# Gram matrices of two samples per matmul, another order of the pieces, and gathers without the wait for gram matrices

## The chip, the cores and the metric

The kernel runs on one core of a Trainium2 chip. A core has TensorE (PE in the rows; matmuls), VectorE (DVE), ScalarE (ACT), GpSimd (POOL) and SyncE (SP), each with its own instruction queue, worked off in order, and 16 DMA engines. Engines wait for each other through semaphores only. The metric is the device time of one execution in microseconds. Here it is 626.21 us (median of 3 runs, 625.28 to 627.51).

## What is computed

For each of 2048 rows, 26 table rows of 64 floats are gathered, projected to 128 and layer-normed, mixed from 26 to 32 features and layer-normed again. With the projected dense row they are 33 vectors of 128. All their pairwise products go through a linear layer with layer norm, and three dense layers follow. All is fp32. Cut to what matters:

```
e = stack([tbl_f[ids[:, f]] for f in range(26)], axis=1)          # (2048, 26, 64)
x = layer_norm(dense @ Wd.T, gd, bd)                              # (2048, 128)
y = layer_norm(einsum('bnd,ed->bne', e, Ws), gs, bs)
y = layer_norm(einsum('bne,pn->bep', y, Wsi), gsi, bsi)           # (2048, 128, 32)
T = concatenate([x[:, None, :], swapaxes(y, 1, 2)], axis=1)       # (2048, 33, 128)
Z = einsum('bnd,bmd->bnm', T, T)
out = layer_norm(Z[:, TRIL_I, TRIL_J] @ Wl.T, gl, bl)             # first 384 of 512 kept
h = relu(concatenate([out, dense], axis=1) @ W_top1 + b_top1)
h = relu(h @ W_top2 + b_top2)
return h @ W_top3
```

## The kernel before

The 2048 rows are 16 tiles of 128. Each tile passes a pipeline of stages, and the program is one loop over "quarters" `h`. A stage that runs once per tile has a number `at`: it runs for tile t in quarter `h = 4t + at` (`tile(h, at)`). A stage that runs in four parts (four batches of features, or four pieces of 32 rows each) runs part k in quarter `4t + at + k` (`part(h, at)`). So four quarters are one tile, and in each quarter every engine does its share for several tiles at once. The order of the calls in the loop body of an engine is the order of that engine's queue. Written out for one tile:

- GpSimd gathers the 26 features by one indirect DMA each (L255), in batches of 8, 6, 6, 6, into one of two buffers `emb`. Before a batch of tile t it waits that the tile two before has been normalized (`nrm_ready`), and that a gram piece has been done (`gram_done`).
- Measuring (part at 1): TensorE transposes a batch (L312), ScalarE copies it (`embt`), TensorE multiplies with a weight gram matrix (L321), VectorE multiplies with `emb` and sums (L757, L761): variances. ScalarE takes the root.
- VectorE normalizes a half of the features (L778, 7 or 6 instructions of two features, written into `nrm` with feature as the fastest index) and shuffles them by 32x32 transposes into `byn` (L788, two instructions), in quarter 5.
- Pieces (part at 6): TensorE mixes (L330), ScalarE copies (`mixed`, L505), TensorE projects (L342), VectorE adds the bias (L793), ScalarE squares (L510), VectorE sums (L800), ScalarE takes the root (L515); in the next quarter VectorE takes the reciprocal (L805) and scales into `V` (L811).
- Gram matrices (part at 7): for each of 32 samples of a piece, one matmul of 32 stationary and 34 moving columns (L354), four samples side by side in four column groups of the array. ScalarE copies the result to `zs` (L521).
- By sample (at 12): VectorE transposes `zs` to `zb` (L822 to L825), TensorE transposes on (L384 to L388), ScalarE copies `zt`. Interact (at 13, L396): the big layer, 5 matmuls of 512 columns. ScalarE squares and scales (`z`), TensorE transposes back (at 15, L404).
- Layer 1 in two halves (at 18 and 19, L418), layer 2 (at 20, L425), layer 3 (at 21, L434), store (at 22). There are 4 * 15 + 23 = 83 quarters.

Each matmul of the source is two instructions of the trace, a transpose is one. The weights are prepared during quarters 0 to 10 (`prepare_...`, `fold`).

## Time and profile before

| | us |
|---|---|
| median of 3 runs | 626.21 |
| the profiled execution | 628.74 |
| its span, first to last instruction | 626.9 |
| TensorE busy in the span | 520.4 |
| VectorE busy | 519.8 |
| ScalarE busy | 295.3 |
| GpSimd busy (making gathers) | 402.9 |

The profiled execution is 2.5 us above the median, and its span 1.8 us below its own time. Two engines are each busy for 83% of the span. The chain of work that ended last is 37% TensorE, 24% VectorE, 16% time without a wait that the profile shows, 8% ScalarE and 8% GpSimd. GpSimd's busy time leaves out a pause of 0.30 us that follows each gather.

### The profile page before, as it was taken

What the parts mean: (1) busy time and instruction counts of PE and PEld (TensorE: products, weight loads), DVE (VectorE), ACT (ScalarE), POOL (GpSimd) and SP (SyncE); (2) the same over time, 40 slices, a digit from 0 to 9 for tenths busy, and PEclk for the clock granted to TensorE, in tenths of its full rate; (3) what the DMA queues carried; (4) which work ended last, traced back from release to release, by engine and by line L of the source; (5) the groups of instructions that cost most, each with busy time, mean ns of one, the idle gap of its engine ahead of it and who ended that gap; (6) DMA issues with size and microseconds to landing.
All of it is one profiled execution on the core that took longest, in us unless ns stands there. A gap on an engine that the chain in (4) does not pass through costs nothing.

```text
span 626.9 us, 17592 instructions
## 1 busy us (share of the span) xinstructions
PE 520.4 (83%) x6955; PEld 394.3 (63%) x6955; DVE 519.8 (83%) x1073; ACT 295.3 (47%) x730; POOL 402.9 (64%) x422
## 2 busy tenths in 40 slices
PE   1462777777899999999998899899998989979886
PEld 1352556545576767676767677676776676747665
DVE  3499689899999999999998979999999898986500
ACT  0410343445465556464636445555555464635422
POOL 6777775767777777777777777777777777200000
PEclk9955887798999999999999899999999999999999
DMA  7311111111111111111111111111111111000000
GB/s 176 109 24 33 27 28 30 28 34 27 35 28 36 28 37 27 37 28 31 34 28 36 29 36 27 37 27 37 28 36 28 29 27 28 14 1 2 2 1 1
DMA packets 22610, 20.22 MB, mean 32 GB/s; under 512 B 12017, under 2 KB 14721, under 8 KB 22529
## 3 DMA queue, kind: packets, MB, share of 16 engines
q0 software_dynamic: 13312, 13.66, 12.1%
q1 hardware_dynamic: 8400, 4.33, 2.7%
q8 instruction: 55, 0.90, 0.6%
q10 hardware_dynamic: 816, 1.11, 0.6%
q14 instruction: 27, 0.21, 0.1%
HBM read 19.07 MB, written 0.01 MB: 30 GB/s over the span
## 4 chain that ended last, share of the span: by engine, by line
PE 37%; DVE 24%; issue 16%; ACT 8%; POOL 8%; DMA 3%; SPq 2%; ACTq 0%; DVEq 0%; POOLq 0%
PE b_l L418 10%; POOL emb L255 8%; PE b_y L342 7%; PE b_l L396 5%; DVE nrm L778 3%; DVE byn L788 3%; DVE V L811 3%; DVE yb L793 3%; DVE var_y L800 3%; PE b_a L321 3%; PE b_z L354 3%; DVE prod L757 2%; DMA emb<-in_tbl,idx 2%; ACT mixed L505 2%; PE b_a L312 2%
## 5 line engine op out<-in xcount | busy, mean ns | idle before, releaser
L255 POOL DMA_INDIRECT emb<-in_tbl,idx x416 | 402.2, 967 | 134.7 <-issue 118.5
L510 ACT ACTIVATE sq<-yb 128x1024 f32<-128x1024 f32 x64 | 67.7, 1059 | 191.1 <-DVE yb L793 187.2
L342 PE MATMUL b_y<-mixed,projw 64*128 64x512 f32 x256 | 74.9, 663 | 23.8 <-ACT mixed L505 23.8
L793 DVE TENSOR_TENSOR yb<-b_y,bias_y 128x1024 f32<-128x1024 f32 x64 | 78.1, 1220 | 19.9 <-PE b_y L342 19.5
L811 DVE TENSOR_TENSOR V<-yb,rstd_y 128x256 f32<-128x256 f32 x256 | 91.9, 422 | 2.2
L800 DVE TENSOR_REDUCE var_y<-sq 128x32 f32<-128x1024 f32 x64 | 77.8, 1215 | 6.9 <-ACT sq L510 5.6
L396 PE MATMUL b_l<-wlt,zt 128*128 128x512 f32 x160 | 72.9, 603 | 0.5 <-ACT zt L561 0.5
L330 PE MATMUL b_mix<-mix,byn 128*128 128x128 f32 x512 | 72.4, 287 | 0.0
L321 PE MATMUL b_a<-gram_w,embt 128*128 128x128 f32 x416 | 66.3, 303 | 6.3 <-ACT embt L494 5.6
L354 PE MATMUL b_z<-V 128*32 128x34 f32 x4096 | 58.2, 200 | 12.5 <-DVE V L811 9.7
L330 PEld LDWEIGHTS b_mix<-mix,byn 128*128 128x128 f32 x512 | 66.4, 203 | 0.2
L354 PEld LDWEIGHTS b_z<-V 128*32 128x32 f32 x4096 | 49.1, 110 | 24.9 <-DVE V L811 9.3
L321 PEld LDWEIGHTS b_a<-gram_w,embt 128*128 128x128 f32 x416 | 57.5, 211 | 11.5 <-ACT embt L494 10.2
L788 DVE STREAM_TRANSPOSE byn<-nrm 128x1024 f32<-128x1024 f32 x32 | 59.3, 1927 | 0.5
L312 PE MATMUL b_a<-ident,emb 128*128 128x128 f32 x208 | 38.5, 303 | 22.4 <-DVE prod L757 16.1
L494 ACT ACTIVATE embt<-b_a 128x512 f32<-128x512 f32 (+1 forms) x64 | 33.0, 516 | 49.6 <-PE b_a L312 49.3
L396 PEld LDWEIGHTS b_l<-wlt,zt 128*128 128x128 f32 x160 | 29.1, 190 | 42.9 <-issue 42.1
L418 PE MATMUL b_l<-z_t,w 128*128 128x128 f32 x384 | 54.1, 278 | 0.0
L778 DVE TENSOR_TENSOR nrm<-emb,rstd_n 128x128 f32<-128x128 f32 x208 | 51.9, 384 | 1.1
L418 PEld LDWEIGHTS b_l<-z_t,w 128*128 128x128 f32 x384 | 48.9, 195 | 0.0
L418 PE MATMUL b_l<-dt,w 128*128 128x128 f32 x256 | 41.6, 286 | 0.9 <-ACT y_sb L596 0.9
L312 PEld LDWEIGHTS b_a<-ident,emb 128*128 128x128 f32 x208 | 25.6, 153 | 26.0 <-issue 18.1
(131 smaller groups left out, 681.7 us busy)
## 6 DMA issues: line engine op xcount, KB each, us to landing
emb<-in_tbl,idx POOLq DMA_INDIRECT x416
dense<-in_r_dense_t SPq DMA_DIRECT2D x16, 128.0 KB, 2.3
...
out_y<-y_sb SPq DMA_DIRECT2D x16, 0.5 KB
...
```

What stands on the lines that cost most here:

```text
L255: pool.indirect_dma_start(out=emb[t % 2][:, f, :], out_offset=None, in_=tables[f], in_offset=bass.IndirectOffsetOnAxis(ap=idx[:, t, f:f + ...
L312: last = nc.tensor.transpose(b_a[:, n * P:(n + 1) * P], emb[t % 2][:, 2 * c:2 * c + 2, :].rearrange("p n d -> p (n d)"), ident[:, :])
L321: last = nc.tensor.matmul(b_a[:, n * P:(n + 1) * P], embt[:, n, :], gram_w[:, :], start=True, stop=True)
L330: last = nc.tensor.matmul(b_mix[:, m * P:(m + 1) * P], byn[t % 2][:, j:j + 2, :].rearrange("p j d -> p (j d)"), mix[:, :], start=True, sto ...
L342: last = nc.tensor.matmul(b_y[:, j2, :], projw[r, :], mixed[c % 2][r, :], start=True, stop=True, tile_position=(64 * j2, 0))
L354: last = nc.tensor.matmul(b_z[32 * q:32 * q + 32, GRAM * j:GRAM * (j + 1)], v[:, 0:NP], v, start=True, stop=True)
L396: last = nc.tensor.matmul(b_l1[:, :], zt[:, c, :], wlt[:, c, :], start=(c == 0), stop=(c == RC - 1))
L418: last = nc.tensor.matmul(dst, w1[:, c, m * P:(m + 1) * P], rhs, start=(n == 0), stop=(n == 4))
L788: nc.vector.transpose(byn[t % 2][:, :, d].rearrange("p j d -> p d j"), nrm[:, d, :]).then_inc(byn_ready, 1)
L793: nc.vector.tensor_tensor(yb[c % 2][:, :, :, :].rearrange("e h s p -> e (h s) p"), b_y[:, :, :].rearrange("e h (s p) -> e (h s) p", p=NP), ...
L800: nc.vector.tensor_reduce(var_y[c % 2][:, :], sq[:, :, :, :].rearrange("e h s p -> e (h s) p"), AXX, ALU.add).then_inc(vary_done, 1)
L811: last = nc.vector.tensor_tensor(V[t % 2][:, j2, c, m:m + 2, :, 0:NP].rearrange("e m q p -> e (m q) p"), yb[c % 2][:, j2, 4 * m:4 * m + 8, :],
```

## The change

- **Gathers** (GpSimd): no wait for `gram_done` any more; a wait for `nrm_ready` remains at the first feature of each half.
- **Gram matrices**: `V` holds two samples side by side (68 columns). One matmul has 64 stationary and 68 moving columns; of the 2x2 blocks the two diagonal ones are used. 16 matmuls per piece in two column groups, where 32 in four were. Their result is in two PSUM banks. ScalarE copies it by 4 instructions on 32 partitions each, where one on 128 was, and writes the dense row's share into `V` by 4 instructions where one was. To make room, the bank `b_l0` is now the bank `b_x`.
- **Layouts**: `nrm` and `zs` have the transposed order of their free dimensions. So L778 writes contiguous runs, and the 32x32 transposes read with a stride. The third transpose of `by_sample` has 128 columns, where 64 were, and TensorE adds its two halves by an accumulating matmul (`pair_x`).
- **Order**: shuffle at 4 (was 5), mix at 5 (was 6), scale in the quarter of its piece, by_sample and pairs at 11 (was 12), interact at 12 (13), back at 14 (15), both halves of layer 1 and layer 2 at 15 (18, 19 and 20), layer 3 at 16 (21), store at 18 (22). 79 quarters. The order within a quarter is new on TensorE, ScalarE and VectorE.

```diff
-        nrm = sb("nrm", [P, D, NP])
+        nrm = sb("nrm", [P, NP, D])
...
-        V = [sb(f"V{h}", [P, 2, 4, 4, NQ, GRAM]) for h in range(2)]
-        zs = [sb(f"zs{h}", [P, GRAM, NJ]) for h in range(2)]
-        zb = sb("zb", [P, ZB_X + 2 * NP])
+        V = [sb(f"V{h}", [P, 4, 2, 4, 2, PAIRED]) for h in range(2)]
+        zs = [sb(f"zs{h}", [P, NJ, SLOTS]) for h in range(2)]
+        zb = sb("zb", [P, ZB_X + 4 * NP])
...
+        b_l0 = b_x
...
-                for b in range(4):
-                    after(pool, nrm_ready, 2 * (t - 2) + b // 2 + 1)
-
-                    after(pool, gram_done, 4 * t + b - PROJECT - 2)
-                    for f in features(b):
-                        pool.indirect_dma_start(out=emb[t % 2][:, f, :], out_offset=None, in_=tables[f],
-                                                in_offset=bass.IndirectOffsetOnAxis(ap=idx[:, t, f:f + 1], axis=0)
-                                                ).then_inc(gathered[t % 2][b], 16)
+                for f in range(NF):
+                    if f in (HALVES[0][0], HALVES[1][0]):
+                        after(pool, nrm_ready, 2 * (t - 2) + (f > 0) + 1)
+                    b = next(b for b in range(4) if f in features(b))
+                    pool.indirect_dma_start(out=emb[t % 2][:, f, :], out_offset=None, in_=tables[f],
+                                            in_offset=bass.IndirectOffsetOnAxis(ap=idx[:, t, f:f + 1], axis=0)
+                                            ).then_inc(gathered[t % 2][b], 16)
...
-                    for q in range(NQ):
-                        v = V[t % 2][:, j % 2, c, j // 2, q, :]
-                        last = nc.tensor.matmul(b_z[32 * q:32 * q + 32, GRAM * j:GRAM * (j + 1)], v[:, 0:NP], v, start=True, stop=True)
+                    for q in range(2):
+                        v = V[t % 2][:, c, j % 2, j // 2, q, :]
+                        last = nc.tensor.matmul(b_z[64 * q:64 * q + 64, j // 4, PAIRED * (j % 4):PAIRED * (j % 4 + 1)], v[:, 2:2 + 2 * NP], v,
+                                                start=True, stop=True, tile_position=(0, 64 * q))
...
+            def pair_x(t):
+                pe.wait_ge(zt_copied, 2 * t + 1)
+                pe.wait_ge(x_copied, 2 * (t + 1))
+                for k in range(2):
+                    nc.tensor.matmul(b_x[0:64, 0:P], zb[:, ZB_X + 64 * k:ZB_X + 64 * (k + 1)], ident[:, :], start=(k == 0), stop=(k == 1),
+                                     tile_position=(0, 0))
...
-                after(pe, h1_relued, 4 * (t - 1) + 2)
-                after(pe, y_copied, t - 1)
+                pe.wait_ge(xn_done, min(t + 4, T))
+                after(pe, y_copied, t)
...
-                    pe.wait_ge(zt_copied, 2 * min(t + 2, T))
-                    after(pe, y_copied, t)
-                else:
-                    pe.wait_ge(z_ready, min(t + 2, T))
+                    pe.wait_ge(x_copied, 2 * min(t + 4, T))
...
-                if (t := tile(h, DENSE_BACK)) is not None:
+                if (x := part(h, 1)):
+                    transposes(*x)
+                if (x := part(h, 6)):
+                    project(*x)
...
+                if (t := tile(h, 14)) is not None:
+                    interact_back(t)
...
+                if (x := part(h, 5)):
+                    mix_features(*x)
+                if (t := tile(h, 15)) is not None:
+                    layer1(t, 0)
...
+                if (t := tile(h, 15)) is not None:
+                    layer1(t, 1)
+                if (x := part(h, 7)):
+                    gram(*x)
...
+                if (t := tile(h, 12)) is not None:
+                    interact(t)
...
-                if (t := tile(h, PAIRS)) is not None:
-                    pair_rows(t)
-                if (t := tile(h, INTERACT)) is not None:
-                    interact(t)
-                if (t := tile(h, LAYER3)) is not None:
-                    layer3(t)
-                if (t := tile(h, LAYER1)) is not None:
-                    layer1(t, 0)
-                if (t := tile(h, INTERACT_BACK)) is not None:
-                    interact_back(t)
-                if (t := tile(h, LAYER1 + 1)) is not None:
-                    layer1(t, 1)
...
-                nc.scalar.activation(zs[t % 2][:, :, 8 * c:8 * c + 8].rearrange("p c j -> p j c"),
-                                     b_z[:, 0:8 * GRAM].rearrange("p (j c) -> p j c", c=GRAM), ACT.Copy).then_inc(zs_copied, 1)
+                for q in range(NQ):
+                    r, slot, first = slice(32 * q, 32 * q + 32), 2 * (q % 2), GRAM * (q % 2)
+                    last = nc.scalar.activation(
+                        zs[t % 2][r, 8 * c:8 * c + 8, slot:slot + GRAM].rearrange("p (a j) c -> p a j c", a=2),
+                        b_z[r, :, 0:4 * PAIRED].rearrange("p a (j c) -> p a j c", c=PAIRED)[:, :, :, first:first + GRAM], ACT.Copy)
+                last.then_inc(zs_copied, 1)
...
-                nc.scalar.activation(V[t % 2][:, :, :, :, :, NP].rearrange("e h c m q -> e q (c m) h"),
-                                     src.rearrange("e (q a h) -> e q a h", q=NQ, h=2), ACT.Identity, scale=gd[:, 0:1], bias=bd[:, 0:1]
-                                     ).then_inc(x_copied, 1)
+                for q in range(NQ):
+                    last = nc.scalar.activation(V[t % 2][:, :, :, :, q // 2, 2 * (NP + 1) * (q % 2)].rearrange("e c h m -> e c m h"),
+                                                src[:, 32 * q:32 * q + 32].rearrange("e (c m h) -> e c m h", m=4, h=2),
+                                                ACT.Identity, scale=gd[:, 0:1], bias=bd[:, 0:1])
+                last.then_inc(x_copied, 1)
...
-                    last = nc.vector.tensor_tensor(nrm[:, :, f:f + 2].rearrange("p d n -> p n d"), emb[t % 2][:, f:f + 2, :],
+                    last = nc.vector.tensor_tensor(nrm[:, f:f + 2, :], emb[t % 2][:, f:f + 2, :],
...
-                for k in range(2):
-                    d = slice(k * D // 2, (k + 1) * D // 2)
-                    nc.vector.transpose(byn[t % 2][:, :, d].rearrange("p j d -> p d j"), nrm[:, d, :]).then_inc(byn_ready, 1)
+                d = slice(k * D // 2, (k + 1) * D // 2)
+                nc.vector.transpose(byn[t % 2][:, :, d].rearrange("p j d -> p d j"), nrm[:, :, d].rearrange("p n d -> p d n")).then_inc(byn_ready, 1)
...
+                if (x := half(h, 2)):
+                    bound_n(*x)
...
+                if (x := part(h, 6)):
+                    scale(*x)
...
+                if (t := tile(h, 4)) is not None:
+                    shuffle(t, 0)
+                    shuffle(t, 1)
```

Three places in the order of the queues. First TensorE at the end of the program, the last two tiles' layers. L396 is interact, L434 layer 3, L418 layer 1, L404 the transposes back, L425 layer 2. Before:

```order
L396 MATMUL b_l<-wlt,zt 128x512 x5
L434 MATMUL b_l<-h,w3p 128x128 x2
L418 MATMUL b_l<-dt,w 128x128 x2
L418 MATMUL b_l<-z_t,w 128x128 x3
L418 MATMUL b_l<-dt,w 128x128 x2
L418 MATMUL b_l<-z_t,w 128x128 x3
L404 MATMUL b_l<-ident,z 128x128 x3
L418 MATMUL b_l<-dt,w 128x128 x2
L418 MATMUL b_l<-z_t,w 128x128 x3
```

and now, where L383, L390 and L392 are the pair transposes, L400 interact, L408 back, L419 layer 1, L426 layer 2, L434 layer 3:

```order
L383 MATMUL b_x<-ident,zb 128x128 x4
L426 MATMUL b_l<-h,w 128x128 x8
L390 MATMUL b_x<-ident,zb 64x128 x2
L392 MATMUL b_x<-xt,ones 32x128
L434 MATMUL b_x<-h,w3p 128x128 x2
L400 MATMUL b_l<-wlt,zt 128x512 x5
L408 MATMUL b_x<-ident,z 128x128 x3
L419 MATMUL b_x<-dt,w 128x128 x2
L419 MATMUL b_x<-z_t,w 128x128 x3
```

Before, all of layer 1 of tile 14 (the four L418 rows behind L434, and the four behind L404) stands behind the last tile's interact. Now even its layer 2 and layer 3 (the rows L426 and L434) stand ahead of it, and behind it follow only the last tile's own layers.

Second VectorE in the middle of the program, in the quarter in which a tile is shuffled. Before:

```order
L800 TENSOR_REDUCE var_y<-sq 128x32
L774 RECIPROCAL rstd_n<-std_n 128x12
L778 TENSOR_TENSOR nrm<-emb,rstd_n 128x2x64 x6
L788 STREAM_TRANSPOSE byn<-nrm 128x32x32 x2
L805 RECIPROCAL rstd_y<-std_y 128x32
L811 TENSOR_TENSOR V<-yb,rstd_y 128x8x32 x4
L793 TENSOR_TENSOR yb<-b_y,bias_y 128x1024
L757 TENSOR_TENSOR prod<-b_a,emb 128x512
```

and now, with L832, L803, L811, L837, L843 and L820 for L800, L774, L778, L805, L811 and L788:

```order
L832 TENSOR_REDUCE var_y<-sq 128x32
L803 RECIPROCAL rstd_n<-std_n 128x12
L811 TENSOR_TENSOR nrm<-emb,rstd_n 128x128 x6
L837 RECIPROCAL rstd_y<-std_y 128x32
L843 TENSOR_TENSOR V<-yb,rstd_y 128x4x64 x4
L820 STREAM_TRANSPOSE byn<-nrm 128x32x32 x2
L825 TENSOR_TENSOR yb<-b_y,bias_y 128x1024
L787 TENSOR_TENSOR prod<-b_a,emb 128x512
```

The scaling of the piece (`V`) moved from behind the two shuffle transposes to ahead of them, and `yb` of the next quarter now stands right behind them.

Third ScalarE in the quarter in which the dense row is written to `V`. Before:

```order
L551 ACTIVATE V<-b_x,bd,gd 128x4x16x2
L554 ACTIVATE xt<-b_x,bd,gd 128x128
L494 ACTIVATE embt<-b_a 128x384
L515 ACTIVATE std_y<-var_y,eps 128x32
L505 ACTIVATE mixed<-b_mix 128x512
L521 ACTIVATE zs<-b_z 128x8x34
L510 ACTIVATE sq<-yb 128x1024
L500 ACTIVATE std_n<-var_m,eps 128x12
L592 ACTIVATE h<-b_l,b 128x128 x2
```

and now:

```order
L503 ACTIVATE embt<-b_a 128x384
L567 ACTIVATE V<-b_x,bd,gd 128x4x4x2 x4
L571 ACTIVATE xt<-b_x,bd,gd 128x128
L532 ACTIVATE zs<-b_z 32x8x34 x4
L607 ACTIVATE h<-b_x,b1p 128x128 x2
L519 ACTIVATE sq<-yb 128x1024
L607 ACTIVATE h<-b_l,b1p 128x128 x2
L576 ACTIVATE zt<-b_x 128x512
L514 ACTIVATE mixed<-b_mix 128x512
L524 ACTIVATE std_y<-var_y,eps 128x32
```

Ahead of the square of the piece (`sq`, L510, now L519) stood six instructions, `mixed` among them. Now ten copies and the first half of layer 1 (`h`, L607) stand ahead of it, and `mixed` has moved behind it, behind the second half of layer 1 and `zt`.

## Rows read from the trace of the kernel before

**Rows 1.** The page's part 2, GpSimd: busy tenths in 40 slices of the span.

```profile
POOL 6777775767777777777777777777777777200000
```

**Rows 2.** Waits of GpSimd over the span: us in total, times, longest us.

```profile
POOL emb L255 <- issue: 118.5, 388, 0.6
POOL emb L255 <- PE b_z L354: 14.3, 26, 3.6
```

**Rows 3.** Timeline of GpSimd: start us, us, engine, line, what [idle before <-releaser].

```profile
3.08 1.10 POOL L255 DMA_INDIRECT emb<-in_tbl,idx  x1 [1.61 <-DMA idx<-in_ids]
...
99.53 0.94 POOL L255 DMA_INDIRECT emb<-in_tbl,idx  x1 [3.63 <-PE b_z L354]
...
175.74 1.03 POOL L255 DMA_INDIRECT emb<-in_tbl,idx  x1 [1.50 <-PE b_z L354]
...
537.31 1.11 POOL L255 DMA_INDIRECT emb<-in_tbl,idx  x1 [0.30 <-issue]
```

**Rows 4.** Windows, one tile and the end: us, busy of PE, PEld, DVE, ACT, POOL, PEclk.

```profile
427.80:460.40 32.60, 30.43 (x435) 23.03 (x431) 30.58 (x62) 18.38 (x45) 24.68 (x27) 1.00 0.16 32
541.80:625.40 83.60, 70.05 (x850) 53.57 (x849) 38.42 (x71) 33.28 (x83) 0.00 (x0) 0.98 0.01 1
```

**Rows 5.** Timeline of TensorE, steady state, then the last batch and the end.

```profile
435.05 0.77 PE L354 MATMUL b_z<-V 128*32 128x34 f32 x64
...
439.74 0.61 PE L418 MATMUL b_l<-dt,w 128*128 128x128 f32 x4
...
442.07 0.98 PE L354 MATMUL b_z<-V 128*32 128x34 f32 x64
...
447.09 2.05 PE L425 MATMUL b_l<-h,w 128*128 128x128 f32 x16
...
454.51 4.56 PE L396 MATMUL b_l<-wlt,zt 128*128 128x512 f32 x10
...
541.81 0.49 PE L312 MATMUL b_a<-ident,emb 128*128 128x128 f32 x3
...
624.37 0.71 PE L434 MATMUL b_l<-h,w3p 128*128 128x128 f32 x4 [0.72 <-ACT h L592]
```

**Rows 6.** Timeline of VectorE, one quarter with a shuffle.

```profile
447.20 1.23 DVE L793 TENSOR_TENSOR yb<-b_y,bias_y 128x1024 f32<-128x1024 f32 x1
448.35 0.55 DVE L757 TENSOR_TENSOR prod<-b_a,emb 128x384 f32<-128x384 f32 x1
...
449.60 1.22 DVE L800 TENSOR_REDUCE var_y<-sq 128x32 f32<-128x1024 f32 x1
450.73 0.22 DVE L774 RECIPROCAL rstd_n<-std_n 128x12 f32<-128x12 f32 x1
450.99 1.58 DVE L778 TENSOR_TENSOR nrm<-emb,rstd_n 128x128 f32<-128x128 f32 x6
452.60 3.80 DVE L788 STREAM_TRANSPOSE byn<-nrm 128x1024 f32<-128x1024 f32 x2
456.27 0.28 DVE L805 RECIPROCAL rstd_y<-std_y 128x32 f32<-128x32 f32 x1
...
457.93 1.22 DVE L793 TENSOR_TENSOR yb<-b_y,bias_y 128x1024 f32<-128x1024 f32 x1
```

**Rows 7.** Groups by line, VectorE with small and with strided operands: busy us, mean ns.

```profile
L714 DVE TENSOR_REDUCE u<-V 128x64 f32<-128x1024 f32 x2 | 3.8, 1896 | 0.1
L825 DVE STREAM_TRANSPOSE zb<-zs 128x64 f32<-128x64 f32 x16 | 3.2, 202 | 0.0
```

**Rows 8.** Groups by line, ScalarE's copies: busy us, mean ns.

```profile
L521 ACT ACTIVATE zs<-b_z 128x272 f32<-128x272 f32 x64 | 41.0, 641 | 0.0
L505 ACT ACTIVATE mixed<-b_mix 128x512 f32<-128x512 f32 x64 | 37.6, 588 | 7.3 <-PE b_mix L330 6.4
L551 ACT ACTIVATE V<-b_x,bd,gd 128x128 f32<-128x128 f32 x16 | 9.4, 588 | 7.3 <-PE b_x L377 7.3
L580 ACT ACTIVATE z_t<-b_l 128x384 f32<-128x384 f32 x16 | 7.8, 490 | 10.7 <-PE b_l L418 10.7
```

300 lines of the change are left out of this document (159 added, 141 removed).

## The prediction, made before the result was known

> **What bounds the kernel now.** I read four views, in this order. The slices of GpSimd [rows 1] are level at 7 tenths up to slice 34 and empty after it. So there are two parts: one in which gathers are made, up to some 540 us, and an end without any. GpSimd's waits [rows 2] say how full the first part is. A gather takes 0.94 us or a little more and is followed by a pause of 0.30 us, which the waits call "issue". The waits for a gram matrix (PE b_z) hold that same pause: 14.3 - 26 x 0.30 = 6.5 us is real waiting. The timeline has the largest, 3.63 us at 99.53, and the last that is more than the pause, 1.50 us at 175.74 [rows 3]. From the first gather (3.08) to the start of the last (537.31) it is 534.2 us for 415 steps, 1.287 us each; without the 6.5 us it is 1.272, or 33.1 us per tile of 26. The third view, one tile in the steady state [rows 4], shows that the other engines just keep up: 32.6 us, TensorE busy for 30.4 of it, VectorE for 30.6. So in the first part three engines are bound at once, and the gathers come first. The last batch's transposes start at 541.81 us [rows 5], 4.5 us after the start of the last gather: the engines are at GpSimd's heels. The fourth view is the end [rows 4]: 83.6 us from there to the end of TensorE's work, TensorE busy for 70.05 of it. It is the part that a new order can shorten.
>
> **The wait of the gathers.** Removed: at most 6.5 us, all of it before 180 us. What waits remain, on `nrm_ready`, don't bind: two buffers are some 33 us of lead, and a half is normalized two or three quarters, about 20 us, behind its gathers. The last gather then starts at 537.3 - 6.5 = 530.8, and its transposes at 535.3 if the engines follow as closely. That is a floor of this kernel: no order of the others gets below it.
>
> **Gram matrices.** In layer 1 twenty instructions of 128 moving columns take 442.07 - 439.74 = 2.33 us [rows 5], 0.91 ns a column. A gram piece is 64 instructions of 34 columns in 0.7 to 0.98 us [rows 5], 11 to 15 ns each, where one alone would stream for 31: between two and three of the four column groups run at once. Now it is 32 instructions of 68 columns, 62 ns each, in two groups: 32 x 62 / 2 = 0.99 us if both groups are full. Bounds: 0.4 us, if it is the number of instructions that counts, and 1.98 us, if the groups don't overlap. I take 1.0, since the row is a matter of columns in two or three groups: +0.2 us a piece.
>
> The Trainium skill (TensorEngine Tiling (Array Packing), Instruction Overhead) says that a matmul has an overhead of some 60 cycles, so that one column costs as much as 60. By it half the instructions would halve a piece, 0.4 us, and the forecast would be about 2 us lower. The rows of this trace, at 11 to 15 ns an instruction, don't show such a floor in four groups.
>
> **ScalarE.** A copy of 272 elements takes 641 ns now, with a strided write [rows 8]. From 384 elements in 490 and 512 in 588 ns [rows 8], 0.77 ns an element, 272 contiguous ones take 0.40 us, and four overlapped some 1.25 us: +0.6 a piece. Bounds 1.2 and 4 x 0.64 = 2.6. The copy to `V`, 588 ns now, becomes four of 32 elements: some 1.1 us, bounds 0.6 and 2.4. ScalarE goes from 18.4 busy us per tile [rows 4] to 21.3, far from the bound, but its queue couples the others.
>
> **VectorE.** L778 writes contiguous runs: 1.61 us for six [rows 6], of which I take off 0.2; 0.4 us a tile. The shuffle's read gets a stride of 256 bytes. A transpose of 64 elements, contiguous on both sides, takes 202 ns, and two of 1024 take 3.67 us [rows 6, 7], 1.8 ns an element in both cases, although the latter write with a stride. So transposes run at some 1.8 ns whatever the layout, and I take 0 for the strided read. The other bound is a reduction: over strided data 1896 ns [rows 7], over contiguous 1.22 us [rows 6], both 1024 elements, +0.68 us. That would be 1.4 us for the shuffle and 0.7 for `by_sample`.
>
> The Trainium skill (SBUF — State Buffer, the note on cachelines under Door 1) speaks against this part: an access that leaves its 16-byte line pays. It is the rule behind the fourth case below, 2.1 us a tile. The strided reduction agrees with it, the transposes with a strided write don't.
>
> **A lap of the steady state.** The sums aren't enough, since order decides. I follow one tile, from the start of the quarter with layer 1 (0), by the starts of the rows [rows 5, 6] and the new order. TensorE: project waits for `mixed` at 1.3, ends 2.4; norms 3.2, mix 4.1, layer 1 8.7, gram 9.7, pair rows 10.1, layer 2 12.0, pair_x 12.8 (with 0.3 for its second matmul). Next quarter: transposes and project, 14.2. VectorE: bias 1.15, norms and bound 1.25, variance 1.15, normalize 1.55, scale 1.7, shuffle 3.7: 24.7 (24.6 with the gain of L778). Meanwhile TensorE has done interact (4.4 us) by 22.1. Next quarter on VectorE: bias, norms and variance 3.6, 0.3 of waiting, scale 1.7: 30.3. Then bias to 31.45, ScalarE squares by 32.7, `mixed` by 33.55, and the next lap's project starts where 1.3 was. **32.2 us a lap**, to which I add 0.3 for small gaps: 32.5. GpSimd needs 33.1. So the engines follow still, with 0.6 us a tile to catch up; and the quarter with layer 1, where the square stands behind it, costs nothing yet, since the chain runs over TensorE there.
>
> The weights' preparation fills VectorE until some 128 us, as before; tile 3's first transposes, which without waits could run at 114, start at about 127. From there 12 laps and 22.9 us to the last batch: 127 + 12 x 32.5 + 22.9 = 540. The floor of the gathers was 535. I take **540**, 1.8 us earlier than now.
>
> **The end.** Same hand work from the last batch's transposes (0). VectorE has shuffled tile 15 by 12.0. Pieces then cost VectorE 5.4 us each (bias 1.15, square 1.1, variance 1.15, root 0.35, scale 1.7): 17.4, 22.8. The third has layer 1 of tile 13 in its quarter, 31.4; the fourth is at 37.3. Interact of tile 14 ends 38.7, and the last piece follows it: project 39.8, scaled 45.1, gram 46.2. Then TensorE alone: layer 1 of tile 14 50.8, pairs and layer 2 53.8, layer 3 and interact 58.8, norm, back and copy 61.5, layer 1 66.1, layer 2 with two copies 69.4, layer 3 and the last copy 70.5. Before it was 83.6: **13 us less**. Nearly 9 of them are work that now lies before the last batch: layer 1 once (4.6), layer 2 twice (2 x 1.9), layer 3 once (0.55). The cover for it in the first part is TensorE's slack, 33.1 - 30.7 us a tile; were it gone, those 9 us would come back there.
>
> **The sum.** Span: 540 + 70.5 + 1.5 for what lies behind TensorE's last instruction = 612.0 us, against 626.9. The profiled execution's own time is its span + 1.8, and the median 2.5 below it: 612.0 + 1.8 - 2.5 = **611.3 us**. Its own range is 604.5 to 617: floor of the gathers and a few us less in the end, or a lap of 33.0.
>
> **Rivals.**
> - *Gathers alone bound it.* If the lap is below 32.2, as with a gram piece of 0.4 us, the last batch is at 535.3: 606.6 us. For it: two chains of 0.6 us slack. Against it: the engines start tile 3 some 12 us late and must make up all of it.
> - *The engines fall behind the gathers.* A gram piece of 1.6 us, or ScalarE's four copies at 2.4 (the copies stand ahead of the square in every quarter), puts 0.6 to 1.1 us on the lap: 33.1 to 33.6, 547 to 553 for the last batch, 618 to 625 us. Then GpSimd waits on `nrm_ready` for the first time.
> - *Slower: the strided reads of VectorE.* At 0.68 us per 1024 elements the shuffle, which is on the chain, is 1.4 us longer and `by_sample` 0.7. With part of the latter on the chain too the lap is 34.3, the last batch at 561, the end 0.7 longer: 633.5 us. It decides from a lap of 33.9 on, that is from 1.4 us more a tile.
> - *It does nothing.* The wait removed was no wait for most of the time, and the order's gain in the end comes back as a longer first part: 624.5 to 628.
>
> **Chances.** Forecast 0.55, gathers alone 0.15, engines behind 0.15, slower by strided reads 0.08, nothing 0.07. A measurement of this kernel tells 0.3%, 1.9 us, from no change. Faster 0.84, same 0.07, slower 0.09. The range takes in the first three: 603 to 624.
>
> **What would show it.** Right: the last gather starts at 531 to 537, a tile's period is 32.5 to 33.1, the last batch's transposes start near 540, and from there it is 70 us. The floor: if transposes follow the gathers at once all along. Wrong: a shuffle transpose above 2.0 us, a gram piece above 1.3, the four copies above 1.6, or waits on `nrm_ready` in GpSimd's list. What I trust least is the lap: 0.3 us in it are 4 us in the result.

## The result and the profile after

The changed kernel takes 639.01 us (median of 4 runs, 637.85 to 639.22), the kernel before 626.62 us (4 runs, 625.28 to 627.51): a ratio of 1.0196, with a 95% interval of 1.0173 to 1.0219. It is 12 us slower where 15 us less were forecast. The profiled execution has a span of 636.8 us, 9.9 more than before. The medians are 12.4 us apart. Most of the other 2.5 us is chance: the profiled execution before (628.74 us) lay 2.1 us above its median, that of the changed kernel (638.92 us) lies at its own.

The waits of GpSimd over the span (us in total, times, longest), which answer to [rows 2], the last gather, the counterpart of [rows 3], and the last batch's transposes on TensorE, that of [rows 5]:

```profile
POOL emb L250 <- issue: 126.5, 415, 0.3
...
531.13 0.94 POOL L250 DMA_INDIRECT emb<-in_tbl,idx  x1 [0.30 <-issue]
...
557.71 0.55 PE L306 MATMUL b_a<-ident,emb 128*128 128x128 f32 x3
```

The gathers did what was forecast: no wait but the pause, and the last one at 531.13 us. But the last batch's transposes start 26.6 us behind it, where they were 4.5 behind before. GpSimd runs ahead, and the other engines set the time.

Two windows, one tile and the end (us, busy of PE, PEld, DVE, ACT, POOL, PEclk, DMA share, GB/s), against [rows 4]:

```profile
425.10:458.80 33.70, 32.01 (x306) 24.24 (x307) 30.61 (x61) 22.73 (x59) 25.70 (x27) 1.00 0.16 31
557.70:635.30 77.60, 64.67 (x541) 48.07 (x540) 37.13 (x65) 37.53 (x93) 0.00 (x0) 0.93 0.00 1
```

A tile takes 33.7 us, and TensorE is busy for 32.0 of them, 1.6 more than before. The last batch stands at 557.7 instead of 541.8 (+15.9), the end is 77.6 us instead of 83.6 (-6.0). The sum is the 9.9 us of the span.

The groups by line (busy us, mean ns of one, idle time before), against [rows 7, 8] and the groups of gram matrices and shuffle transposes:

```profile
L532 ACT ACTIVATE zs<-b_z 32x272 f32<-32x272 f32 x256 | 98.9, 386 | 4.0 <-PE b_z L348 1.7
L348 PE MATMUL b_z<-V 128*64 128x68 f32 x2048 | 76.6, 229 | 4.3 <-ACT zs L532 3.4 <-DVE V L843 0.9
L820 DVE STREAM_TRANSPOSE byn<-nrm 128x1024 f32<-128x1024 f32 x32 | 69.3, 2219 | 0.0
...
L811 DVE TENSOR_TENSOR nrm<-emb,rstd_n 128x128 f32<-128x128 f32 x208 | 45.1, 286 | 1.1
```

The same groups of the kernel before read:

```profile
L788 DVE STREAM_TRANSPOSE byn<-nrm 128x1024 f32<-128x1024 f32 x32 | 59.3, 1927 | 0.5
L354 PE MATMUL b_z<-V 128*32 128x34 f32 x4096 | 58.2, 200 | 12.5 <-DVE V L811 9.7 <-issue 2.6
L778 DVE TENSOR_TENSOR nrm<-emb,rstd_n 128x128 f32<-128x128 f32 x208 | 51.9, 384 | 1.1
```

Half as many gram matmuls are busy for 76.6 us instead of 58.2, and a shuffle transpose takes 2.22 us instead of 1.93: both above what was taken. Of the four signs that the prediction named for being wrong, only one came, a shuffle transpose above 2.0 us. A gram piece stayed below its bound (1.09 us from start to start in the steady state, against 1.3), the four copies too (1.58 against 1.6), and there were no waits on `nrm_ready`.

### The profile page after: what moved, and what is told of

Its sections match the earlier page's. It is cut to its first block, busy times and chain, and to the rows that moved or that the text cites. A ratio compares the mean times of both kernels' runs of the same rounds, so it can differ in the third digit from the quotient of the medians.

```text
span 636.8 us, 13843 instructions
## 1 busy us (share of the span) xinstructions
PE 550.4 (86%) x4955; PEld 415.6 (65%) x4955; DVE 529.1 (83%) x1081; ACT 372.7 (59%) x970; POOL 402.8 (63%) x422
## 4 chain that ended last, share of the span: by engine, by line
PE 38%; DVE 37%; issue 17%; ACT 4%; SPq 2%; DMA 1%; DVEq 0%; ACTq 0%
DVE byn L820 7%; PE b_x L419 6%; PE b_l L419 6%; DVE V L843 6%; PE b_y L336 5%; PE b_l L426 5%; DVE prod L787 4%; DVE yb L825 4%; DVE var_y L832 4%; DVE nrm L811 3%; DVE var_n L791 3%; PE b_z L348 3%; PE b_a L315 3%; PE b_mix L324 2%; DVE rstd_y L837 2%
## 5 line engine op out<-in xcount | busy, mean ns | idle before, releaser
L532 ACT ACTIVATE zs<-b_z 32x272 f32<-32x272 f32 x256 | 98.9, 386 | 4.0 <-PE b_z L348 1.7
L843 DVE TENSOR_TENSOR V<-yb,rstd_y 128x256 f32<-128x256 f32 x256 | 92.3, 423 | 2.2
L519 ACT ACTIVATE sq<-yb 128x1024 f32<-128x1024 f32 x64 | 67.7, 1058 | 29.3 <-DVE yb L825 29.3
L832 DVE TENSOR_REDUCE var_y<-sq 128x32 f32<-128x1024 f32 x64 | 77.6, 1212 | 4.7 <-ACT sq L519 4.7
L315 PEld LDWEIGHTS b_a<-gram_w,embt 128*128 128x128 f32 x416 | 55.8, 205 | 38.7 <-ACT embt L503 35.5
L503 ACT ACTIVATE embt<-b_a 128x512 f32<-128x512 f32 (+1 forms) x64 | 32.5, 508 | 82.7 <-PE b_a L306 82.7
L348 PE MATMUL b_z<-V 128*64 128x68 f32 x2048 | 76.6, 229 | 4.3 <-ACT zs L532 3.4
L348 PEld LDWEIGHTS b_z<-V 128*64 128x64 f32 x2048 | 67.8, 139 | 13.0 <-issue 4.8
L324 PEld LDWEIGHTS b_mix<-mix,byn 128*128 128x128 f32 x512 | 64.4, 197 | 11.6 <-DVE byn L820 10.8
L400 PE MATMUL b_l<-wlt,zt 128*128 128x512 f32 x160 | 71.6, 594 | 0.0
L820 DVE STREAM_TRANSPOSE byn<-nrm 128x1024 f32<-128x1024 f32 x32 | 69.3, 2219 | 0.0
L400 PEld LDWEIGHTS b_l<-wlt,zt 128*128 128x128 f32 x160 | 29.1, 190 | 30.8 <-issue 30.6
L811 DVE TENSOR_TENSOR nrm<-emb,rstd_n 128x128 f32<-128x128 f32 x208 | 45.1, 286 | 1.1
L336 PEld LDWEIGHTS b_y<-mixed,projw 64*128 64x128 f32 x256 | 19.9, 190 | 34.4 <-ACT mixed L514 27.0
L787 DVE TENSOR_TENSOR prod<-b_a,emb 128x512 f32<-128x512 f32 (+1 forms) x64 | 37.0, 578 | 5.8 <-PE b_a L315 5.8
L837 DVE RECIPROCAL rstd_y<-std_y 128x32 f32<-128x32 f32 x64 | 22.4, 349 | 23.0 <-ACT std_y L524 23.0
```

The costliest lines, as they stand in the source:

```text
L315: last = nc.tensor.matmul(b_a[:, n * P:(n + 1) * P], embt[:, n, :], gram_w[:, :], start=True, stop=True)
L324: last = nc.tensor.matmul(b_mix[:, m * P:(m + 1) * P], byn[t % 2][:, j:j + 2, :].rearrange("p j d -> p (j d)"), mix[:, :], start=True, sto ...
L336: last = nc.tensor.matmul(b_y[:, j2, :], projw[r, :], mixed[c % 2][r, :], start=True, stop=True, tile_position=(64 * j2, 0))
L348: last = nc.tensor.matmul(b_z[64 * q:64 * q + 64, j // 4, PAIRED * (j % 4):PAIRED * (j % 4 + 1)], v[:, 2:2 + 2 * NP], v, start=True, stop= ...
L400: last = nc.tensor.matmul(b_l1[:, :], zt[:, c, :], wlt[:, c, :], start=(c == 0), stop=(c == RC - 1))
L532: last = nc.scalar.activation(zs[t % 2][r, 8 * c:8 * c + 8, slot:slot + GRAM].rearrange("p (a j) c -> p a j c", a=2), b_z[r, :, 0:4 * PAIR ...
```

## The experiments

The theories. **A**: the added work lies on the chain of the lap and makes it longer: the strided read of the shuffle, the gram matrices in pairs with what goes with them. **B**: the new order itself makes a longer lap. **C**: the wait that was removed had a use.

### The parts apart, with gathers

`e1`, `e7` and `e14` are the kernel before with one line taken out:

```diff
-                    after(pool, gram_done, 4 * t + b - PROJECT - 2)
```

`e2` and `e8` are the changed kernel with the old layout of `nrm`:

```diff
-        nrm = sb("nrm", [P, NP, D])
+        nrm = sb("nrm", [P, D, NP])
...
-                nc.vector.transpose(byn[t % 2][:, :, d].rearrange("p j d -> p d j"), nrm[:, :, d].rearrange("p n d -> p d n")).then_inc(byn_ready, 1)
+                nc.vector.transpose(byn[t % 2][:, :, d].rearrange("p j d -> p d j"), nrm[:, d, :]).then_inc(byn_ready, 1)
```

`e3`, `e9` and `e12` are the changed kernel with gram matrices of one sample, and the old `V`, `zs`, `zb`, their copies and `pair_x`; `e4`, `e10`, `e11` and `e13` have both, so that of the change only the order (with `b_l0` in the bank of `b_x`) and the missing wait are left:

```diff
-                    for q in range(2):
-                        v = V[t % 2][:, c, j % 2, j // 2, q, :]
+                    for q in range(NQ):
+                        v = V[t % 2][:, j % 2, c, j // 2, q, :]
```

> The kernel before, with only the gathers' wait for gram matrices taken out. If the gathers bound the first part, the last gather starts some 6.5 us earlier (531 instead of 537.3) and the time falls by up to 6.5 us, to 620. If the other engines are the bound (in the changed kernel GpSimd never waited and it gained nothing), the last gather starts earlier but the last batch's transposes stay near 541.8, and the time stays within 0.3% of 626.6.

> The changed kernel with the old layout of nrm: L778 writes with a stride again, the shuffle reads contiguous runs. Theory A (the strided read of the shuffle lengthens the lap of the steady state, since the shuffle is on its chain): two shuffle transposes fall from 4.23 to 3.67 us, six or seven nrm instructions rise by 0.2 to 0.3, so the lap falls by some 0.3 to 0.5 us from 33.55 and the time by 4 to 7 us, to 632 to 635. Theory B (the order alone makes the lap): no change beyond 2 us.

> The changed kernel with gram matrices of single samples again (V, zs and zb as before, 64 instructions of 34 columns, one copy to zs and one to V, one transpose in pair_x), new order and new nrm layout kept. Theory A (added work per piece, on ScalarE's queue 0.94 us and on TensorE 0.3 us, by_sample 0.3 us): the lap falls by 0.6 to 1.0 us and the time by 8 to 13 us, to 626 to 631. Theory B (the order makes the lap): less than 3 us.

> The new order and the gathers without the wait alone: gram matrices of single samples and the old nrm layout. Theory A: the lap is that of my hand trace, 32.2 to 32.9 (then the gathers bound it), and with the shorter end the time is 612 to 622 us, below the kernel before. Theory B (the order itself puts TensorE's layer quarter and VectorE's shuffle quarter one behind the other): lap 33.0 or more, 626 us or more.

What came was expected by none. On this chip the kernel before took 810.34 us (9 runs, 807.62 to 812.19), and the four took 1024.24 (ratio 1.265, 1.261 to 1.269), 996.80 (1.229, 1.226 to 1.232), 1020.82 (1.255, 1.248 to 1.262) and 1024.54 us (1.264, 1.261 to 1.268). All four lack the wait of the gathers. So the changed kernel itself came next, and the same with the wait put back:

```diff
+                    if f == features(b)[0]:
+                        after(pool, gram_done, 4 * t + b - 8)
```

> The changed kernel, unchanged, as the control for the four runs before it, all of which leave out the gathers' wait for gram matrices and took 997 to 1025 us on a chip on which the kernel before takes 810. If the missing wait costs 190 us on a chip of that kind (theory C: gathers issued back to back starve TensorE of something), this one too takes about 1000 us there (ratio 1.23 to 1.27), and on a chip where the kernel before takes 626 us it takes 639 (ratio 1.02).

> The changed kernel with the wait put back: the gathers of a batch again wait until the gram matrices eight pieces earlier stand in b_z. Theories A (the added work in the lap) and B (the new order itself) expect what the changed kernel gives, ratio 1.02, on a chip where the kernel before takes 626 us, or a little more: there the gathers run some 26 us ahead at the end, so that they have slack for the wait. Theory C expects that on a chip of the slow kind it takes back most of the 190 us (a ratio of about 1.02 to 1.05 instead of 1.23), and on the other kind gains up to 3 us, if the gathers' distance was worth anything there.

Another chip came up, on which the kernel before took 627.43 us (7 runs). The changed kernel took 639.43 us (638.76 to 640.11; ratio 1.0192, 1.0149 to 1.0235), as at first, and with the wait 636.96 (636.77 to 637.27; ratio 1.0152, 1.0110 to 1.0194). The runs of the two don't overlap: the wait is worth 2.5 us there, of which the traces show 0.9 us in the laps (from tile 2 on all are 33.4 us with the wait; without it three of the thirteen are 33.6 to 33.7), 1.1 us behind the last shuffle and no cause that I could name. It doesn't explain the 12 us.

The parts were then run again:

> The kernel before with its gathers' wait taken out, once more, now beside the kernel before on a chip of the kind on which that takes 626 us (on the other it took 1024 against 810). Theory C (the missing wait itself costs, since gathers back to back disturb TensorE) expects 630 to 640 us here too; theories A and B expect 617 to 627: the gathers' last start moves from 537 to about 531, and the engines, whose lap is 32.2 us, then end when they end.

> The changed kernel with the old layout of nrm, once more on such a chip: the shuffle's transposes read contiguously again (2 x 1.92 instead of 2 x 2.22 us in each lap) and the normalization writes strided (8 x 0.38 instead of 8 x 0.29 us). Theory A expects a lap shorter by what lies on VectorE's way to the next projection, 0 to 0.6 us, so 629 to 639 us; theory B expects no more than 0.1 us a lap: 637 to 639.

> The changed kernel with gram matrices of one sample again (one zs copy a piece instead of four, old V copy, old zs and zb), the new order and nrm kept, once more on such a chip. Theory A expects the lap to fall from 33.5 to about 32.7 us (ScalarE's 0.94 us a piece and the gram's 0.3 us a piece lie on the chain), so 625 to 632 us; theory B expects 633 to 641, since VectorE and TensorE stand as they did and the gram of one sample is no longer on TensorE than that of two.

> The order alone with the wait taken out, old gram, zs, V and nrm, once more on such a chip. Theory A expects 612 to 622 us: with none of the added work the order gives what it was forecast to give. Theory B (the order itself makes the lap, because in its last quarter VectorE's transposes, ScalarE's copies and TensorE's layer stand one behind the other) expects 630 to 640 us.

> The order alone with the wait taken out, old gram, zs, V and nrm, looked at once more in surroundings in which the kernel before takes 626 us, if they come up. Theory A (the added work makes the lap) expects 612 to 622 us, laps of 32.2 us; theory B (the order itself) 630 to 640 us, laps of 33.3 us and more. Where the kernel before takes 808 us, it comes out at 1025 again and tells nothing of A against B.

> The changed kernel with gram matrices of one sample (one zs copy a piece, old V copy, zs and zb), new order and new nrm. Theory A expects a lap of about 32.7 us, 625 to 632 us; theory B 633 to 641 us, laps of 33.3 us and more. Against the order alone it shows what the strided shuffle read costs: 0.56 us a lap by theory A, that is 7 to 9 us of the time; nothing by theory B. Where the kernel before takes 808 us, it comes out at 1015 to 1021 again.

> The order alone with the wait taken out, old gram, zs, V and nrm. Where the kernel before takes 626 us: theory A (the added work makes the lap) expects 612 to 622 us and laps of 32.2 us; theory B (the order itself makes it) 630 to 640 us and laps of 33.3 us and more. Where the kernel before takes 808 us: 1025 again, since this kernel lacks the wait (theory C).

> The kernel before with its gathers' wait taken out. Where the kernel before takes 626 us, theory C expects 628 to 631: the changed kernel gained 2.5 us there from having the wait back, and the same disturbance should show here; theories A and B, for which the wait is only a hold-up of the gathers, expect 617 to 627. Where it takes 808 us: 1024 again.

Only other chips came up, three with the first one, and on each the kernel before took 798 to 810 us. Measured: `e7` 1023.27 us (ratio 1.270, 1.257 to 1.284), `e8` 997.91 (1.243, 1.231 to 1.255), `e9` 1015.08 (1.264, 1.252 to 1.277), `e10` 1027.62 (1.278, 1.267 to 1.289), `e11` 1023.93 (1.266, 1.261 to 1.272), `e12` between 1005.25 and 1022.78 in its four runs, too far apart for a ratio (beside the same runs of the kernel before as `e11`, 809.20), `e13` 1019.16 (1.278, 1.264 to 1.293), `e14` 1012.14 (1.273, 1.259 to 1.287). On these chips one line, the wait of the gathers, is worth more than 200 us: theory C is shown there, by `e1`, `e7` and `e14`. How the wait does it was not seen, since there is no trace of the kernel with the wait on such a chip. The group of the gram matmuls in `e14` (busy us, mean ns of one, idle time before):

```profile
L353 PE MATMUL b_z<-V 128*32 128x34 f32 x4096 | 112.1, 205 | 188.4 <-issue 180.4
```

TensorE idles 188 us before these instructions, 180 of them waiting for nothing that the profile shows. In the kernel before, on the chip of the first comparison, it was 12.5 us, 2.6 of them without a visible wait. Matmuls of one piece, the last gather of a tile, and the next piece, in the timeline of `e14`:

```profile
602.52 0.25 PE L353 MATMUL b_z<-V 128*32 128x34 f32 x3 [1.15 <-issue]
...
611.91 0.95 POOL L254 DMA_INDIRECT emb<-in_tbl,idx  x1 [0.31 <-issue]
...
623.72 0.32 PE L353 MATMUL b_z<-V 128*32 128x34 f32 x10
623.95 0.72 PE L353 MATMUL b_z<-V 128*32 128x34 f32 x54
```

While gathers are made without a break, the matmuls of a piece come a few at a time, these three after a pause of 1.15 us. Once GpSimd stands, the next piece runs as one, 64 of them in under 1 us. The same kernel in two windows, with gathers and after the last of them (`e1`; columns as above):

```profile
560.00:620.00 60.00, 39.06 (x438) 29.99 (x437) 29.96 (x60) 18.65 (x45) 24.97 (x26) 0.78 0.09 18
900.00:960.00 60.00, 52.66 (x745) 38.67 (x735) 52.37 (x102) 31.45 (x76) 0.00 (x0) 0.97 0.01 2
```

Without gathers VectorE does 102 instructions in the time in which it did 60. The granted clock is lower too beside the gathers, 0.78 against 0.97, but it isn't what makes the time: a gram matmul takes 205 ns in `e14` and 200 in the kernel before on the first chip, and the 188 us are idle time. That hid the question at hand, but it also answers it: each of these kernels has one full lap behind its last gather. From the start of the shuffle of tile 14 to that of tile 15 it is 31.93 us in `e14`, and 32.04 in `e13`, whose rows are:

```profile
915.47 3.74 DVE L807 STREAM_TRANSPOSE byn<-nrm 128x1024 f32<-128x1024 f32 x2
947.51 3.65 DVE L807 STREAM_TRANSPOSE byn<-nrm 128x1024 f32<-128x1024 f32 x2
```

In `e12` (new `nrm`, single samples) the same lap is 32.54 us, in `e8` (pairs, old `nrm`) 32.86. The repeats agree within 0.03 us: 31.92 to 31.93 in `e1`, `e7` and `e14`, 32.03 to 32.06 in `e4`, `e10`, `e11` and `e13`, 32.54 to 32.55 in `e3`, `e9` and `e12`, 32.84 and 32.86 in `e2` and `e8`. So the new `nrm` adds 0.50 us to the order alone and the pairs add 0.81. Theory B had 33.3 for the order alone; these laps say 32.0.

### Stages in one kernel

The next kernel holds order and added work in stages, so that one run would do:

```diff
+FOUR_FROM, STRIDED_FROM = 6, 10
...
+                n = 8 if t < FOUR_FROM else 2
+                for j in range(0, 8, n):
+                    last = nc.scalar.activation(zs[t % 2][:, :, 8 * c + j:8 * c + j + n].rearrange("p c j -> p j c"),
...
+                src = nrm[:, d, :] if t < STRIDED_FROM else nrm2[:, :, d].rearrange("p n d -> p d n")
```

> One kernel with three stages, each laps long enough to read: the new order (no gathers' wait) with the old gram matrices, zs, V and nrm for tiles 0 to 5; from tile 6 the zs copy of a piece in four activations (2 of its 8 columns each, same data) and the V copy in four; from tile 10 also nrm in its new layout, a second buffer, with the strided read of the shuffle. Where the kernel before takes 626 us: theory B (the order itself makes the lap) expects laps of 33.3 us or more in all three stages; theory A (added work) 32.2 us in the first, about 32.8 in the second if ScalarE's copies are on the way, and 0.5 more in the third from the strided read, which leaves the rest of the changed kernel's 33.5 to the gram of pairs. In all 620 to 640. Where the kernel before takes 808 us: about 1020, and the stages tell nothing.

On a fourth chip of the kind on which the kernel before takes 800 us it took 1017.21 us (ratio 1.272, 1.266 to 1.277), and the laps of the first two stages tell nothing. The lap behind the last gather is one of the third stage, and has 32.53 us.

### Without the gathers

Since the laps behind the last gather are undisturbed on any chip, the last three kernels make no gathers from tile 2 on; the embeddings of tiles 0 and 1 are used again, so their output means nothing, and all other work stays:

```diff
-            for t in range(T):
+            for t in range(2):
...
-                pe.wait_ge(gathered[t % 2][b], 16 * len(features(b)) * (t // 2 + 1))
+                pe.wait_ge(gathered[t % 2][b], 16 * len(features(b)))
```

> The kernel before without the gathers from tile 2 on (emb of tiles 0 and 1 is used again, so the output is not the reference's; all the work of the engines stays). In the eleven runs of kernels without the wait the one full lap after the last gather was undisturbed: 31.9 to 32.0 us for the order before, 32.0 for the new order alone. Theory C (back-to-back gathers hold TensorE up on these chips) expects all laps here at 31.9 to 32.0 us and about 612 us in all on any chip; if something else of these chips is slow, laps of 40 us and more stay.

> The changed kernel without the gathers from tile 2 on. Theory A (added work) expects laps of 33.4 us, 1.4 more than without it, and some 14 x 1.4 = 20 us less 6 us for the shorter end more than the kernel before without its gathers: ratio 1.02 to 1.03. A theory by which the gathers' share makes the difference (they run back to back in the changed kernel, and share ports and queues with the engines) expects 32.0 to 32.5 us a lap here and a ratio of 0.99 to 1.005.

> The three stages without the gathers from tile 2 on: the new order with the old work for tiles 0 to 5, zs and V copies split in four from tile 6, nrm in its new layout and the strided read of the shuffle from tile 10. Theory A expects laps of 32.0, 32.0 to 32.6 and 0.5 more; theory B (the order makes the lap) 33.3 in all three. What then lacks to the changed kernel's 33.4 is the gram of pairs on TensorE with its wider zs to zb transposes.

Beside each other on a fifth such chip, with the kernel before at 808.35 us: `e16` 663.25 us (6 runs, 659.11 to 664.52; ratio 0.820, 0.817 to 0.823), `e17` 684.46 (681.38 to 685.51; ratio 0.847, 0.844 to 0.850), `e18` 666.00 (663.29 to 668.17; ratio 0.825, 0.822 to 0.828). The 612 us expected for `e16` missed: the gathers of the first two tiles still disturb the head, and the first shuffle starts at 101.8 us, not at 57.4. The ratio of `e17` to `e16` is 1.032, just above the 1.02 to 1.03 expected, for a longer head. From tile 3 on all laps are alike. Two successive shuffles in `e16`, in the first, second and third stage of `e18`, and in `e17`:

```profile
521.70 3.71 DVE L788 STREAM_TRANSPOSE byn<-nrm 128x1024 f32<-128x1024 f32 x2
553.68 3.70 DVE L788 STREAM_TRANSPOSE byn<-nrm 128x1024 f32<-128x1024 f32 x2
```

```profile
239.53 3.75 DVE L819 STREAM_TRANSPOSE byn<-nrm 128x1024 f32<-128x1024 f32 x2
271.53 3.74 DVE L819 STREAM_TRANSPOSE byn<-nrm 128x1024 f32<-128x1024 f32 x2
...
335.54 3.73 DVE L819 STREAM_TRANSPOSE byn<-nrm 128x1024 f32<-128x1024 f32 x2
367.53 3.74 DVE L819 STREAM_TRANSPOSE byn<-nrm 128x1024 f32<-128x1024 f32 x2
...
496.45 4.30 DVE L819 STREAM_TRANSPOSE byn<-nrm 128x1024 f32<-128x1024 f32 x2
528.94 4.31 DVE L819 STREAM_TRANSPOSE byn<-nrm 128x1024 f32<-128x1024 f32 x2
```

```profile
511.85 4.32 DVE L820 STREAM_TRANSPOSE byn<-nrm 128x1024 f32<-128x1024 f32 x2
545.24 4.34 DVE L820 STREAM_TRANSPOSE byn<-nrm 128x1024 f32<-128x1024 f32 x2
```

| | lap, us |
|---|---|
| kernel before (`e16`) | 31.98 |
| new order, old work (`e18`, tiles 4 and 5) | 32.00 |
| and `zs` and `V` copies split in four (tiles 7 and 8) | 31.99 |
| and the new `nrm` with the strided read (tiles 12 and 13) | 32.49 |
| the whole change (`e17`) | 33.39 |

Theory B falls: the order is worth nothing in the lap, neither way. Theory A holds: 0.50 us from the layout of `nrm`, 0.90 from the pairs (0.81 in `e2` and `e8`, with the old layout). The split in four is a test of the number of instructions only: four copies of a quarter each take 0.64 us together, as one did. In the changed kernel each of the four covers 272 elements on 32 partitions and they take 1.58 us; that size has no stage of its own.

Where the 0.50 us are, in VectorE's timeline in the quarter of the shuffle, first stage, then third:

```profile
300.48 1.50 DVE L809 TENSOR_TENSOR nrm<-emb,rstd_n 128x128 f32<-128x128 f32 x6
301.82 0.33 DVE L836 RECIPROCAL rstd_y<-std_y 128x32 f32<-128x32 f32 x1
...
303.53 3.75 DVE L819 STREAM_TRANSPOSE byn<-nrm 128x1024 f32<-128x1024 f32 x2
307.12 1.22 DVE L824 TENSOR_TENSOR yb<-b_y,bias_y 128x1024 f32<-128x1024 f32 x1
...
525.99 1.30 DVE L809 TENSOR_TENSOR nrm<-emb,rstd_n 128x128 f32<-128x128 f32 x6
527.21 0.35 DVE L836 RECIPROCAL rstd_y<-std_y 128x32 f32<-128x32 f32 x1
...
528.94 4.31 DVE L819 STREAM_TRANSPOSE byn<-nrm 128x1024 f32<-128x1024 f32 x2
533.16 1.17 DVE L824 TENSOR_TENSOR yb<-b_y,bias_y 128x1024 f32<-128x1024 f32 x1
```

From start to start, the two transposes go from 3.59 to 4.22 us (+0.63), the normalization from 1.34 to 1.22 (-0.12). VectorE has no idle time in this quarter, so the 0.51 us are the lap's.

Where the 0.90 us are, in TensorE's timeline in the quarter with layer 1 and 2, third stage of `e18`, then `e17`:

```profile
517.04 0.77 PE L351 MATMUL b_z<-V 128*32 128x34 f32 x64
517.74 0.66 PE L385 MATMUL b_x<-ident,zb 128*128 128x128 f32 x4
518.23 1.95 PE L426 MATMUL b_l<-h,w 128*128 128x128 f32 x16
520.02 0.27 PE L391 MATMUL b_x<-ident,zb 128*64 128x128 f32 x1
...
520.56 0.55 PE L309 MATMUL b_a<-ident,emb 128*128 128x128 f32 x3
```

```profile
532.47 1.17 PE L348 MATMUL b_z<-V 128*64 128x68 f32 x32
533.56 0.66 PE L383 MATMUL b_x<-ident,zb 128*128 128x128 f32 x4
534.06 1.95 PE L426 MATMUL b_l<-h,w 128*128 128x128 f32 x16
535.94 0.65 PE L390 MATMUL b_x<-ident,zb 128*64 128x128 f32 x4
...
536.85 0.55 PE L306 MATMUL b_a<-ident,emb 128*128 128x128 f32 x3
```

From start to start: the gram piece 0.70 and 1.09 us (+0.39), pair rows 0.49 and 0.50, layer 2 1.79 and 1.88 (+0.09), `pair_x` 0.54 and 0.91 (+0.37). That is 0.86 of the 0.90, one behind the other on TensorE, which has no pause here from the first half of layer 1 to the projection. Only one gram piece of a lap counts so: behind two of the other three the projection waits for `mixed` (0.91 and 1.01 us in the third stage, 0.65 and 0.66 in `e17`), and the longer pieces only shorten these waits. The transposes of `by_sample` cost VectorE 2.63 us instead of 2.30 (1.14, 1.12 and 0.37 against 1.06, 1.04 and 0.20), beside TensorE's layer 1.

The four copies to `zs` stand beside the chain, not on it, but barely. Ahead of TensorE's quarter the chain runs over the square of the piece, which stands behind the copies in ScalarE's queue. Third stage, then `e17`:

```profile
475.17 1.06 ACT L519 ACTIVATE sq<-yb 128x1024 f32<-128x1024 f32 x1 [0.76 <-DVE yb L824]
...
489.70 1.06 ACT L519 ACTIVATE sq<-yb 128x1024 f32<-128x1024 f32 x1
```

From VectorE's bias (473.91 and 488.44) it is 1.26 us to the square in both. ScalarE waited 0.76 us for it in the stage, and doesn't any more in `e17`: the copies have used up the cover.

## Why the prediction was wrong, point by point

**The gathers: the size right, the floor irrelevant.** The last gather at 531.13 was forecast at 530.8, and no wait on `nrm_ready` shows. What failed is "the gathers come first". GpSimd starts a tile of gathers every 33.1 us (499.57 - 3.45 over 15 tiles), as forecast. The engines were to need 32.5 and need 33.5 on average (435.9 us for thirteen laps), so the last batch follows them and not the gathers. Before, it was the other way round: without gathers the engines' lap is 31.98 us, with them 32.1 to 32.2 in most laps, and in the others TensorE stood waiting for a gather, for 2.40 us in the longest. So the engines had about 0.9 us a tile to spare beside the gathers, and the change took 1.4. And the wait was not a mere hold-up: putting it back gains 2.5 us on one chip, and the kernel before loses over 200 us without it on others.

**The lap: the step that failed.** By hand it was 32.2 us, and 32.5 with gaps; `e17` has 33.39, the changed kernel 33.4 to 33.7. The 0.9 us between come from two terms. The strided read was taken as 0, with 0.1 us off for L811, so that the layout would gain 0.1: it costs 0.50, a miss of 0.6. The conclusion "1.8 ns an element in both cases" has two faults. It is miscounted: 202 ns for 64 elements are 3.2 ns an element, against 1.8 in the 1024 that write with a stride, so rows of such different size price no stride at all. And even a free strided write says nothing of a strided read. Measured are 2.22 us per 1024 elements against 1.93, +0.29, less than half of the bound of 0.68 from the reduction. The Trainium skill (SBUF — State Buffer, the note on cachelines) had the sign right: it says that each access that crosses to a new line of 16 bytes pays. The other term is TensorE's quarter: +0.3 for the gram piece and +0.3 for `pair_x` were in the hand lap, 0.86 to 0.90 came, a miss of 0.3. The hand lap itself holds up: with the old work it would have been some 31.7, with my 0.3 for gaps 32.0, and the first stage has 32.00. Over the twelve laps and three quarters up to the last batch, 0.9 us a lap are some 11 us, the largest part of the 27.7 us between 611.3 and 639.0.

**Gram matrices.** Taken 1.0 us, bounds 0.4 and 1.98; measured 1.09 from start to start. The reading by columns in two groups came close. The Trainium skill (TensorEngine Tiling (Array Packing), Instruction Overhead) counts some 60 cycles for each matmul however few its columns; by that rule a piece of half the instructions would be shorter, and it became longer.

**ScalarE.** Four copies 1.25 us, bounds 1.2 and 2.6; measured 1.58. The copy to `V` 1.1, measured 1.21 from the first to the last. Neither is in the 1.41 us: TensorE (0.86) and VectorE (0.51) account for 1.37 of them.

**The head.** Tile 3's first transposes were forecast at 127 and started at 130.8. Between the shuffles of tiles 0 and 2 it is 74.7 us, where it was 69.9. Without gathers the same two laps are 67.9 us before, 73.6 in the order with the old work and 75.2 with the whole change: so most of this, 5.7 us, comes with the order and the bank that it gives up. TensorE waits in `prepare_wlt` for VectorE's `wlt` (the row from TensorE's waits in the changed kernel, then VectorE in the timeline), since `b_l1` is now the only bank for it; behind that wait stand the norms, and VectorE waits for these.

```profile
PE b_l L296 <- DVE wlt L779: 6.7, 3, 2.8
...
108.63 0.56 DVE L787 TENSOR_TENSOR prod<-b_a,emb 128x384 f32<-128x384 f32 x1 [4.50 <-PE b_a L315]
```

That the bank is the cause is argued, not tried: no run had the order with a bank of its own. The prediction had "as before" for this part, and followed no queue in it.

**The last batch.** 540 forecast, 557.7 measured: 3.8 from the head, 13.0 from the twelve laps that followed (33.58 us on average instead of 32.5) and 1.1 from the last three quarters (24.0 instead of 22.9). Of the 1.1 us a lap 0.9 are the terms above; 0.2 come with the gathers, since `e17` has 33.39.

**The end: half of the gain.** 70.5 forecast, 77.6 measured, 83.6 before. The early part went as followed: tile 15 shuffled at 12.6 (12.0), the pieces scaled at 18.3 (17.4), 24.0 (22.8), 32.6 (31.4), 39.0 (37.3), interact of tile 14 done at 40.3 (38.7). Then (changed kernel, TensorE):

```profile
600.68 1.17 PE L348 MATMUL b_z<-V 128*64 128x68 f32 x32 [1.62 <-ACT zs L532]
603.88 0.55 PE L408 MATMUL b_x<-ident,z 128*128 128x128 f32 x3 [2.04 <-ACT z L596]
605.45 2.08 PE L348 MATMUL b_z<-V 128*64 128x68 f32 x32 [1.02 <-ACT zs L532]
607.46 1.22 PE L419 MATMUL b_x<-dt,w 128*128 128x128 f32 x4
...
618.60 4.46 PE L400 MATMUL b_l<-wlt,zt 128*128 128x512 f32 x10
```

The gram matrices wait for ScalarE's four copies, and the granted clock falls: 0.93 on average in this window, 0.98 before. The last piece's gram takes 2.08 us instead of 1.17 and ends at 49.8 instead of 46.2; layer 1 of tile 14 begins at half speed, 1.22 us for what takes 0.61 later. Interact is over at 65.4 instead of 58.8, and the rest takes 12.2 instead of 11.7. In the 10 us before the clock fell (597 to 607) TensorE had been busy for 5.3.

From the start of the last shuffle to the end it is 76.3 us before and 70.7 after. The clock's share can be read from one kernel under two clocks: the order alone takes 70.1 us in `e10` (70.2 and 70.1 in `e4` and `e13`), with a mean granted clock of 0.87 in the first 65 us of it, and 66.8 in `e11`, with 0.92. So the order shortens the end by 6 to 9.5 us, less than the 13 forecast, and 3.3 us of that hang on the clock. The changed kernel has 0.92 there too, as `e11`, and takes 3.9 us more: that is about what its added work costs the end, the waits for the copies in the rows above among it. How these 3.9 us divide wasn't tried.

**The rivals.** By its lap (33.1 to 33.6) what came is the second rival, the engines behind the gathers. Its mechanism is not what came: a gram piece of 1.6 us or four copies at 2.4 were to do it, and they measured 1.09 and 1.58. The strided read of the third rival did more, at less than half of the price given for it, together with 0.3 us more on TensorE than taken. The two were priced as alternatives, and their sum is what happened to the lap. The head (3.8 us) and the end (7.1) had no rival, and 2.9 us more come from the step from the span to the median: the prediction took 2.5 us off, and this profiled execution lay at its median. These 13.8 us carry the result past the range of 603 to 624. The sign given for the second rival, a wait on `nrm_ready`, did not appear although the engines fell behind by 26.6 us: two buffers still cover that.

**What the parts are worth on one chip without gathers.** `e17` less `e16` is 21.2 us, and in the traces 21.0: 0.8 up to the first shuffle, 7.3 in two laps of the head, 18.3 in the thirteen laps, -5.4 at the end. With gathers it is 9.9, since the laps of the kernel before are longer with them: its thirteen laps from the shuffle at 127.3 us to the one at 550.6 are 32.56 us on average. The longest is 35.6 us. TensorE waits in it for a gather, and the granted clock in its window is 0.95 (kernel before, the window, then TensorE):

```profile
352.60:388.20 35.60, 33.49 (x448) 26.19 (x449) 30.20 (x60) 19.19 (x46) 27.07 (x29) 0.95 0.17 32
...
353.06 0.66 PE L312 MATMUL b_a<-ident,emb 128*128 128x128 f32 x4 [2.40 <-DMA emb<-in_tbl,idx]
```
